# A bidirectional Mamba scan on one core: first loads in another order, absent chunks left out, four evictions one exponential later

## The reference

```python
mod = (silu(c) @ wmod).reshape(2, 6, 1, -1)        # sa, ca, ga, sb, cb, gb
h = layernorm(x) * (1 + ca) + sa
fwd, bwd = mamba(h; weights f), flip(mamba(flip(h); weights b))
x = x + ga * (concat(fwd, bwd) @ wproj.T + bproj)
h = layernorm(x) * (1 + cb) + sb
x = x + gb * (mx_quantized(h) @ mx_quantized(weight).T + bias)
# mamba, d_inner 1024, 16 states:
u, z = split(h @ win.T); u = silu(causal_conv4(u) + bconv)
dt, B, C = split(u @ wx.T); delta = softplus(dt @ wdt.T + bdt)
state_t = exp(delta_t * A) * state_{t-1} + delta_t * u_t * B_t     # 16 states per channel
y = (sum_n state * C + u * Dp) * silu(z); out = y @ wout.T
```

## Time and profile before

| | us |
|---|---|
| median of 3 runs | 7422.68 (7402.39 to 7422.73) |
| profiled execution | 7414.95 |
| its span | 7413.2 |
| busy: PE / DVE / ACT / POOL | 6753.6 / 6890.9 / 6151.4 / 6961.1 |
| mean granted TensorE clock | 0.976 of 2.4 GHz |

### The profile page before, as it was taken

How to read it: one execution, slowest core, us unless ns; L and a number is a source line. 1 busy time by engine, 2 the same in 40 slices (tenths; PEclk the granted TensorE clock), 3 DMA queues, 4 the chain that set the end, 5 groups by cost and what they waited for, 6 DMA issues and landing times. The chain is left out here.

```text
span 7413.2 us, 108939 instructions
## 1 busy us (share of the span) xinstructions
PE 6753.6 (91%) x32598; PEld 4030.3 (54%) x32598; DVE 6890.9 (93%) x9252; ACT 6151.4 (83%) x13132; POOL 6961.1 (94%) x3766
## 2 busy tenths in 40 slices
PE   8999999999999998899999899999999999999889
PEld 4555555555555555555555555555555555555455
DVE  6999999999999999999999999999999999999766
ACT  5888888888888888888888888888888888888645
POOL 5999999999999999999999999999999999999678
PEclk9999999999999999999999999999999999999999
DMA  4454444445444444544444454454444544444555
GB/s 163 131 159 138 125 143 140 140 137 157 133 126 141 135 133 128 152 136 116 144 139 133 128 146 140 110 147 138 133 128 143 152 109 144 133 137 129 164 184 171
DMA packets 581024, 1034.51 MB, mean 140 GB/s; under 512 B 100512, under 2 KB 213408, under 8 KB 572256
## 3 DMA queue, kind: packets, MB, share of 16 engines
q1 hardware_dynamic: 576288, 1025.56, 46.6%
q10 hardware_dynamic: 4160, 2.10, 0.1%
HBM read 901.13 MB, written 126.30 MB: 139 GB/s over the span
## 5 line engine op out<-in xcount | busy, mean ns | idle before, releaser
L513 POOL TENSOR_TENSOR dBu<-Bb,du 128x1024 f32<-128x1024 f32 x2048 | 4796.7, 2365 | 2.5 <-DMA Bb<-bc_scratch 2.5
L652 ACT ACTIVATE scans<-delta,A 128x512 f32<-128x512 f32 x4096 | 2744.3, 696 | 233.4 <-DVE hC L1151 223.4
L1135 DVE TENSOR_TENSOR_SCAN scans<-scans,state,dBu 128x512 f32<-128x512 f32 x2016 | 2535.2, 1278 | 226.0 <-ACT scans L652 223.9
L1135 DVE TENSOR_TENSOR_SCAN dBu<-scans,state,dBu 128x512 f32<-128x512 f32 x1568 | 1956.5, 1260 | 7.4 <-ACT scans L652 7.4
L883 PE MATMUL yT<-ident,hC 128*128 128x128 f32 x9216 | 1389.6, 281 | 274.4 <-DVE hC L1151 272.3
L1151 DVE TENSOR_TENSOR hC<-scans,Cb 128x512 f32<-128x512 f32 x2304 | 1553.2, 678 | 2.9 <-PE yT L883 2.8
L525 POOL TENSOR_TENSOR hR<-dBu,Cb 128x512 f32<-128x512 f32 x1024 | 1306.3, 1276 | 216.3 <-DVE dBu L1135 216.0
L883 PEld LDWEIGHTS yT<-ident,hC 128*128 128x128 f32 x9216 | 1077.0, 144 | 568.4 <-DVE hC L1151 345.5
L599 ACT ACTIVATE turned<-bg,CT 128x128 f32<-128x128 f32 x3072 | 877.1, 370 | 246.2 <-PE bg L860 245.6
L876 PE MATMUL bg<-u,comb 128*128 128x512 f32 x2048 | 963.8, 597 | 50.9 <-ACT pre L612 50.0
L834 PE MATMUL bg<-hT,win_z 128*128 128x512 f32 x2048 | 977.7, 600 | 0.0
(11 more groups left out here) (147 smaller groups left out, 7970.2 us busy)
## 6 DMA issues: line engine op xcount, KB each, us to landing
comb<-pre_scratch SPq DMA_DIRECT2D x1024, 256.0 KB, 4.5
Bb<-bc_scratch SPq DMA_DIRECT2D x264, 512.0 KB, 7.0
Cb<-bc_scratch SPq DMA_DIRECT2D x264, 512.0 KB, 7.1
win_u<-in_win SPq DMA_DIRECT2D x264, 256.0 KB, 4.6
win_z<-in_win SPq DMA_DIRECT2D x257, 256.0 KB, 2.7
pre_scratch<-pre SPq DMA_DIRECT2D x256, 256.0 KB, 3.6
comb<-comb_scratch SPq DMA_DIRECT2D x64, 1024.0 KB, 8.2
part_scratch<-pre SPq DMA_DIRECT2D x128, 256.0 KB, 2.0
```

Source lines behind the costliest of these rows:

```text
L513: pool.tensor_tensor(dBu[:, ring(g, q)], Bb[:, 2 * q:2 * q + 2, :], du[:, j % 2, :].unsqueeze(1).broadcast_to([P, 2, T]), ALU.mult).then_i ...
L652: act.activation(place(n)[:], delta[:, j % 2, :], ACT.Exp, scale=A[:, i // CH_DIR, j * N + n:j * N + n + 1]).then_inc(dA_made, 1)
L1135: nc.vector.tensor_tensor_scan(to, place(n)[:], dBu[:, ring(g, q), k, :], state[:, c:c + 1] if i % CH_SEQ else 0.0, ALU.mult, ALU.add).the ...
```

## The change

Four edits. (1) SP's first loads: the small tensors go ahead, `wmod` comes in four row blocks with a semaphore each, and PE makes the modulation with the row block outside. The diagonals of Dp are made and stored before the first rows are normalized. The conv weights' stores, `wgain`, `wproj` and `wout` are issued from ACT's queue between the Silus of the prologue. (2) `made_in` says which names exist in a chunk; U, C, X, K, H and D0 are left out of the last chunk, H and the normalization of rows out of the last two, with their loads and stores. The two table loads of each visit stay. (3) Bank waits come from `user_of_bank_before` in place of the table `LAST`; for all chunks but the first and the last two this gives the same waits. (4) Evictions whose position is a visit's (`LATER`: by the table of positions these are O2 at 15, U1 at 23, C6 at 47, T101 at 53) are taken one exponential later: after the first `step_dA` of the next position, before its second.

```diff
+LATER = [name for name in BY_ACT if TAKE[name] in GATED and TAKE[name] < POS - 1 and name not in URGENT]
+def made_in(i, name):
+    if i == 0:
+        return name[0] != "O" and name != f"Y{MT - 1}"
+    if i == CHUNKS - 1:
+        return name[0] not in "UCXKH" and name != "D0"
+    return i < CHUNKS - 2 or name[0] != "H"
...
             sp.dma_start(cT[:], io["cT"].rearrange("(k p) b -> p k b", p=P)).then_inc(c_loaded, 16)
-            sp.dma_start(wmod, io["wmod"][:, 0:2 * D].rearrange("(k p) n -> p k n", p=P)).then_inc(wmod_loaded, 16)
+            sp.dma_start(skips[:], io["Dp"]).then_inc(small_loaded, 16)
+            sp.dma_start(gtaps[:], io["wconv"]).then_inc(small_loaded, 16)
+            sp.dma_start(bproj[:], io["bproj_columns"]).then_inc(small_loaded, 16)
+            sp.dma_start(A[:], io["Alog"]).then_inc(A_loaded, 16)
+            for k in range(KD):
+                sp.dma_start(wmod[:, k, :], io["wmod"][k * P:(k + 1) * P, 0:2 * D]).then_inc(wmod_loaded[k], 16)
             load_x("x", 0)
...
-                if m == RING:
-                    sp.dma_start(wproj, io["wprojT"][0:D].rearrange("(k p) n -> p k n", p=P)).then_inc(wout_loaded, 16)
-                    sp.dma_start(wout, io["wout"][0].rearrange("(k p) n -> p k n", p=P)).then_inc(wout_loaded, 16)
...
                 act.activation(u[:, 0, m, :], u[:, 0, m, :], ACT.Silu, bias=bconv[:, m:m + 1]).then_inc(u_made, 1)
+                if m == 0:
+                    act.wait_ge(wtaps_made, 2)
+                if m < 2:
+                    act.dma_start(dram["wtap"][m].rearrange("m p c -> p m c"),
+                                  wtaps[:, m].rearrange("p (m j) c -> p m (j c)", j=NG)).then_inc(wtaps_stored, 16)
+                if m == 2:
+                    act.dma_start(wgain[:], io["wmod"][:, 2 * D:3 * D].rearrange("(k p) n -> p k n", p=P)).then_inc(wgain_loaded, 16)
+                if m == 3:
+                    act.dma_start(wproj, io["wprojT"][0:D].rearrange("(k p) n -> p k n", p=P)).then_inc(wout_loaded, 16)
+                if m == 4:
+                    act.dma_start(wout, io["wout"][0].rearrange("(k p) n -> p k n", p=P)).then_inc(wout_loaded, 16)
...
                         if q == 1 and g > 0:
                             take_yT(g - 1, ready(i - 1, "Y6") if j == 0 else ready(i, f"Y{(j - 2) % MT}"))
-                        if p == TAKE[f"D{m}"] + 1:
+                        for name in LATER:
+                            if p == TAKE[name] + 1 and made_in(i, name):
+                                take(name, i, s, g)
+                        if p == TAKE[f"D{m}"] + 1 and made_in(i, f"D{m}"):
                             step_exp(freed(i, f"D{m}"))
...
                         for name in BY_ACT:
-                            if p == TAKE[name] and name not in URGENT and (i > 0 or name not in SKIPPED):
+                            if p == TAKE[name] and name not in URGENT and name not in LATER and made_in(i, name):
                                 take(name, i, s, g)
...
-                        if p == RSTD_AT:
+                        if p == RSTD_AT and i + 2 < CHUNKS:
                             deviation(i + 2)
                         for tt in range(TT):
-                            if p == NORM_POS + tt:
+                            if p == NORM_POS + tt and i + 2 < CHUNKS:
                                 normalize(i + 2, tt)
...
-            pe.wait_ge(wmod_loaded, 16)
-            for m in range(2 * KD):
-                for k in range(KD):
+            for k in range(KD):
+                pe.wait_ge(wmod_loaded[k], 16)
+                for m in range(2 * KD):
                     ins = nc.tensor.matmul(scans[:, 0, m * NB:(m + 1) * NB], wmod[:, k, m * P:(m + 1) * P], cT[:, k, :],
-                                           start=(k == 0), stop=(k == KD - 1))
+                                           start=(k == 0 and m == 0), stop=(k == KD - 1), skip_group_check=True)
```

More of the change, by code:

```diff
@@ L87 @@
 NUM = {name: e for e, name in enumerate(BY_END)}
[L89 to L92, removed]
 URGENT = [f"Z{j}" for j in range(MT)] + ["U3"]
@@ L198, in scan_stage @@
                                                           sem("small_loaded"))
-        wmod_loaded, wgain_loaded = sem("wmod_loaded"), sem("wgain_loaded")
+        wmod_loaded, wgain_loaded = [sem(f"wmod_loaded{k}") for k in range(KD)], sem("wgain_loaded")
         wout_loaded, wout_late_loaded, wproj_late_loaded = (sem("wout_loaded"), sem("wout_late_loaded"),
@@ L229, in scan_stage, with user_of_bank_before @@
         H0, C0, U0, R0, S0, Z0, Y0, DU0 = 2 * AHEAD, HC, HC, HR, 2, 1, 1, 1
+        MADE = [[name for name in BY_END if made_in(i, name)] for i in range(CHUNKS)]
+        TAKEN = [[name for name in BY_ACT if made_in(i, name)] for i in range(CHUNKS)]
+        MADE_TO = [PRO + sum(len(names) for names in MADE[:i]) for i in range(CHUNKS + 1)]
+        TAKEN_TO = [PRO + sum(len(names) for names in TAKEN[:i]) for i in range(CHUNKS + 1)]
+        ALL_READY, ALL_FREED = MADE_TO[CHUNKS], TAKEN_TO[CHUNKS]
         def ready(i, name):
-            if i < 0 or (i == 0 and name in SKIPPED):
-                return PRO
-            return PRO + FIRST_NUM[name] + 1 if i == 0 else (i - 1) * EV + PRO + len(FIRST_NUM) + NUM[name] + 1
+            return MADE_TO[i] + MADE[i].index(name) + 1 if i >= 0 and made_in(i, name) else MADE_TO[max(i, 0)]
         def freed(i, name):
[L239 to L243, removed]
+            return TAKEN_TO[i] + TAKEN[i].index(name) + 1
+        def user_of_bank_before(i, name):
+            users = [other for other, _, bank in SCHEDULE if bank == BANK[name]]
+            at = i * len(users) + users.index(name) - 1
+            while at >= 0 and not made_in(at // len(users), users[at % len(users)]):
+                at -= 1
+            return (at // len(users), users[at % len(users)]) if at >= 0 else (-1, None)
         straight = lambda g, n: g * NS + (len([k for k in STRAIGHT if k < n]) + C0)
@@ L315, in load_BC @@
                                  src.partition_broadcast(P)).then_inc(C_loaded[q], 16)
-                    if q == NQ - 3 and last is not None:
+                    if q == NQ - 3 and last is not None and turned is not None:
                         sp.wait_ge(bg_ready, turned)
@@ L698, in _ @@
             act.wait_ge(consts_made, 3)
+            act.wait_ge(small_loaded, 48)
+            for d in range(2):
+                for m in range(MT):
+                    ins = act.mul(skip_diag[:, d, m, :], ident[:], skips[:, d, m:m + 1])
+                ins.then_inc(skip_made, 1)
+            act.wait_ge(skip_made, 2)
+            for d in range(2):
+                act.dma_start(dram["skip"][d].rearrange("m p c -> p m c"), skip_diag[:, d]).then_inc(skip_stored, 16)
             deviation(0)
@@ L787, in bank_free @@
             def bank_free(i, name):
-                before, earlier = LAST[name]
-                c = i - 1 if earlier else i
-                if i == 0 and before == "O3":
+                c, before = user_of_bank_before(i, name)
+                if i == 0 and name == "U1":
                     pe.wait_ge(comb_taken, MT)
-                    return
-                if 1 <= i <= MT and before == "Z6":
+                elif 1 <= i <= MT and name == "K":
                     pe.wait_ge(comb_taken, MT + i)
-                if before[0] == "Y":
+                elif before is not None and before[0] == "Y":
                     pe.wait_ge(gated, c * MT + (int(before[1:]) + 2 if before != "Y7" else 1))
-                else:
+                elif before is not None:
                     pe.wait_ge(bg_free, freed(c, before))
@@ L921, in background @@
                     for piece in range(len(at)):
-                        if at[piece] != p or (i == 0 and name in SKIPPED):
+                        if at[piece] != p or not made_in(i, name):
                             continue
```

97 lines of the change are left out of this document (39 added, 58 removed).

## The result

The changed kernel takes 7427.07 us (7411.3 to 7440.84, 22 runs), the kernel before 7412.46 us in the same series (7402.39 to 7429.89, 22 runs): ratio 1.0018, 95% interval 1.0011 to 1.0026, which is +8 to +19 us. The forecast was -8. Both are within the 0.3% that was called no change and the time lies inside the range given, but the sign is the other one, and it is measured.

What follows compares the result with a forecast made beforehand. Bound: a ring of waits among PE, ACT, DVE and POOL, with PE late from p = 15 to 29. Sum +18.6 - 18.2 + 8.5 - 10.8 - 5.0 - 1.2 = -8.1 us, so about 7415 on the median 7422.68; range 7380 to 7452.

Steps and rivals of the forecast that it cites:

- PE as the late link from 15 to 29: Positions 15 to 29 of a chunk: the other engines wait for PE, so its delay arrives whole at the visit at 31.
- O2 at +18.6 us: Eviction at p = 15: taken later, it lengthens PE's stall before O3 from 1.61 to 2.2 us, 0.60 us in 31 chunks.
- Five more stretches at 1.2 GHz, +8.5 us: Behind O3's stall: the longer stall drops PE to half clock in 5 more chunks, 1.7 us each; bounds 0 to +44.
- Rival B: Behind O3's stall: clock falls to 1.2 GHz nearly always, 26 more chunks, +44 us instead of +8.5, time 7450; chance 0.17.
- T101, -18.2 us: Eviction at p = 53: taken later, DVE's first scan starts earlier, gaining 0.57 us in 32 chunks; bounds -1.02 and 0 each.
- U1 and C6 at 0: Evictions at p = 23 and 47: no net gain; banks wanted three positions later, covering the 0.60 us delay.
- Prologue, -10.8 us: Before the loop: -10.2 from U3's earlier load, -1.4 from modulation in row blocks, +0.8 from loads sharing ACT's queue.
- The contention: Prologue, ACT's queue: large loads and stores beside the reloads of U4 to U7 cost +0.8 us, bounds 0 and +5.
- The +3 worked out from it: Prologue: by the queue-turn rule, reloads beside `wout` come about a microsecond late for up to three U; kept as warning.
- Last chunks, -6.2 us: Last two chunks: work left out gives -5.0 us in the last (bounds -2, -8), -1.2 in the one ahead (0, -4).
- Rival A: All chunks: PE takes up O2's 0.60 us, DVE's gains stay, no further half clock; -44.5 us, time 7378, chance 0.20.
- rival D: Prologue: it does not get shorter, as ACT's queue takes what SP's gave; +10.8 us, time 7426, chance 0.05.

## Why the prediction was wrong, point by point

- **PE as the late link from 15 to 29, O2 at +18.6 us.** Right. Stall 2.22 us, visits 28.6 us apart at full clock, both as forecast. One place of the path I had missed: the delay meets ACT first at the copy of `yt`, three positions ahead of O3.
- **Five more stretches at 1.2 GHz, +8.5 us.** This is the step that failed. There were 17 more (22 instead of 5), at 1.7 us +29 us, 20 more than put in. I wrote "nearest to the rows is a small step, as the stall grows by a third of its length", as if the share went with the length. It goes from 12% to 74% for those 0.6 us. The earlier trace rows had hinted at it: equal stalls ended both ways, so the kernel stood at an edge, where a small step can move many chunks. Rival B, chance 0.17, had this mechanism; it gave 26 more and 7450; its count was high by 9.
- **T101, -18.2 us.** Right in kind, -12 (-4 to -19) measured alone. In chunks 9 to 30 the visits 53 to 63 are 32.93 us apart instead of 33.72, more than the 0.57 forecast. In chunks 1 to 8 they are 34.79 instead of 34.44 (34.49 in the run with T101 alone): behind the waits of 0.45 and 0.25 us DVE has a further one of 1.2 to 2.5 us in each of them. These eight chunks are the ones in which PE and ACT also make a part of the second direction's combined output weights at p = 52 to 55 (`COMB_LATE`), which the forecast did not look at; that this work is the cause was not tried.
- **U1 and C6 at 0.** Not tried alone. PE waits for ACT ahead of neither C0 nor C7. But the reason given, banks wanted three positions later, is misread: C0 stands at p = 24 and C7 at p = 48, where the moved evictions now stand too.
- **Prologue, -10.8 us.** It gave 7.1 in this pair of executions, and that flatters it. Up to the visit at 15 of chunk 0 the four profiled kernels with the old prologue run the same instructions, and so do eight with the new one and its loads early. The visit stands at 138.3 to 141.4 us in the four (mean 140.3) and at 134.3 to 139.3 in the eight (mean 136.9): 3.4 us are gained. U3's stall went as forecast. U0 is done 4.1 us earlier in this pair, but 2 of these are luck: PE makes U0's eight products 0.44 us apart in this execution and 0.72 in the one before, and either occurs with either prologue (0.44 in 1 of the 4 and 2 of the 8, 0.67 to 0.78 in the others). Like with like, U0 is 1.5 to 2.0 us earlier; forecast was 1.4. The contention is the mis-sized term: +7.0 (2.70 and 4.93 less the 0.33 that DVE idles at each U) instead of +0.8, and beyond its bound of 5; in the eight it is 6.8 to 9.6. 1.7 of it is again the clock: behind its wait PE makes U7's first four products at half speed. The Trainium skill's rule (DMA: Bandwidth & Descriptors, queues, rings and completion order), that engines take turns between queues, was the better guide: the waits went with the loads' move to another time. The +3 worked out from it was too low too.
- **Last chunks, -6.2 us.** Measured -7.5 (chunk 30 -1.1, chunk 31 to the final stage -6.4). Right.
- **Final stage.** Left out of the sum, +2.1 in this pair. It does not stand out: the stage takes 389 to 390 us in the four kernels with the old prologue and 389 to 391.5 in the ten others.

With the sizes of two steps as this pair has them, 29 for 8.5 and in the prologue -10.2 - 4.1 + 7.0 = -7.3 for -10.8, the sum is +18.6 + 29 - 18.2 - 7.3 - 5.0 - 1.2 = +15.9 us, against +11.8 measured. The clock's share is 20 of the 24 us by which the sum has moved. Over all executions it closes less well: with the prologue at -3.4 the sum is +19.8, and the ratio says +13 (+8 to +19). Where the rest lies is open. Rival A (PE takes up the delay) is refuted by every run with a stall, rival D (no gain in the prologue) by the 3.4 us, though two thirds of the forecast gain are missing. A slip in the chances: A's 0.20 and a fifth of 0.45 are 0.29 for faster than 7400, not 0.27.

## What to carry to other kernels

An instruction that empties a bank should be moved by what waits for it, not by who is ahead of it in its own queue: look for the engine that wants the bank next and whether that engine is late there. The cure for such a stall may be one position in the consumer's schedule (here 56 us gained) where moving the eviction later costs 40; moving it ahead of the visit did as well (7319 and 7322 us). If the trace shows equal stalls of TensorE that sometimes end in the slower clock and sometimes not, the kernel is at an edge: count what all of them cost, in both directions, before anything lengthens them. And before a difference of a few microseconds in a prologue is explained, look at the same stretch in every profiled execution that runs it.

## What the runs showed of the hardware that was not expected

- At the place ahead of O3 the granted clock falls to 1.2 GHz in none of 90 chunks without a stall, 15 of 124 with 1.61 us, 46 of 62 with 2.22 us and 29 of 31 with 2.83 us. Each time it costs 1.7 us there, about as much as the stall itself. Between the visits at 53 and 63 it fell more often with fewer stalls (18 chunks against 1), and the time did not change.
- The same instructions run at either clock from one execution to the next: U0's eight products in the prologue came 0.44 us apart in 5 of 14 profiled executions and 0.67 to 0.78 in 9, which moves what follows by 2 us.
- A stall removed on the late path gave back 1.2 us at full clock (28.0 to 26.8) of its 1.61. Where the other 0.4 are waited for was not followed up.
- In the last chunk, with the products for a next chunk gone, the clock is 0.83 in the mean; at most 1.6 us can hang on it, as POOL is busy 150.37 of 152 us there.
